# Ternary feed-forward stage: activations quantised in groups of two, two and four tiles in place of four and four

## The reference

```python
def act_quant(x):                      # per token
    scale = 128 / clip(max(abs(x), axis=-1), 1e-5)
    return clip(round(x * scale), -128, 127) / scale

def weight_quant(w):
    scale = 1 / clip(mean(abs(w)), 1e-5)
    return clip(round(w * scale), -1, 1) / scale

def bitlinear(x, w):   return act_quant(x) @ weight_quant(w).T
def h_bitlinear(x, w): return act_quant(fwht(x)) @ weight_quant(w).T   # fwht: Walsh-Hadamard transform

gate = bitlinear(x, w_gate)            # 1024 tokens, 256 -> 1024
up = bitlinear(x, w_up)
out = h_bitlinear(silu(gate) * up, w_down)
x = x + tanh(g_ffn[1]) * out           # here x on the right of bitlinear is the layernorm of x
```

## Time and profile before

| | us |
|---|---|
| median of 3 runs | 979.94 |
| lowest and highest of them | 978.31, 980.38 |
| the profiled execution | 978.6 |
| its span, first to last instruction | 976.9 |
| the ternary stage in it | 473.1 to 553.0 |

### The profile page before, as it was taken

How to read it: one execution, slowest core, us unless ns; L and a number is a source line. 1 busy time by engine, 2 the same in 40 slices (tenths; PEclk the granted TensorE clock), 3 DMA queues, 4 the chain that set the end, 5 groups by cost and what they waited for, 6 DMA issues and landing times. The chain is left out here.

```text
span 976.9 us, 17508 instructions
## 1 busy us (share of the span) xinstructions
PE 892.1 (91%) x5665; PEld 559.2 (57%) x5672; DVE 704.9 (72%) x1425; ACT 603.3 (62%) x1185; POOL 382.6 (39%) x325
## 2 busy tenths in 40 slices
PE   9799989898999999999499888999789999988868
PEld 4555646424777777776277663333455666666535
DVE  6999988889666676666778778997472334249777
ACT  5799945887777777777466376888414334213643
POOL 2899510586545555554133181000003776410010
PEclk9899999999999999999799999999899999999989
DMA  5333058000000000000000292000052332240001
GB/s 153 133 108 108 2 185 246 12 6 12 20 18 16 22 18 16 21 16 1 6 1 1 83 393 80 3 2 2 1 190 43 76 76 44 44 119 1 1 0 44
DMA packets 43975, 56.77 MB, mean 58 GB/s; under 512 B 5712, under 2 KB 34904, under 8 KB 43912
## 3 DMA queue, kind: packets, MB, share of 16 engines
q1 hardware_dynamic: 39880, 50.44, 15.7%
q0 software_dynamic: 4032, 5.51, 3.3%
HBM read 49.64 MB, written 6.23 MB: 57 GB/s over the span
## 5 line engine op out<-in xcount | busy, mean ns | idle before, releaser
L1511 POOL TENSOR_TENSOR a_scratch<-a_scratch,a_inverse 128x512 f32<-128x512 f32 x64 | 66.6, 1041 | 115.2 <-DVE a_inverse L1647 115.2
L2494 DVE TENSOR_REDUCE a_tops<-bank 128x4 f32<-128x1024 f32 x64 | 77.8, 1223 | 9.5 <-PE bank L2205 6.4
L2750 PE MATMUL bank<-wup,moe_xT 128*128 x184 | 83.0, 594 | 1.2 <-ACT moe_xT L2825 1.1
L2389 ACT ACTIVATE a_room<-bank,exp_scale 128x1024 f32<-128x1024 f32 x64 | 71.2, 1114 | 13.7 <-PE bank L2228 13.7
L587 POOL TENSOR_TENSOR ssm_drive<-ssm_du,ssm_b_row 128x1024 f32<-128x1024 f32 x32 | 74.5, 2355 | 3.4 <-DVE ssm_state L664 2.0
L1428 ACT ACTIVATE a_scratch<-bank,a_bias,a_q_factor 128x256 f32<-128x256 f32 x128 | 71.1, 560 | 7.1 <-DVE a_bias L1634 6.8
L664 DVE TENSOR_TENSOR_SCAN ssm_state<-bank,ssm_drive 128x512 f32<-128x512 f32 x64 | 74.6, 1207 | 0.8 <-POOL ssm_drive L587 0.5
L3018 DVE TENSOR_TENSOR moe_act_f<-bank,moe_silu 128x512 f32<-128x512 f32 x23 | 15.9, 691 | 76.7 <-ACT moe_silu L2832 65.0
L1240 PE MATMUL bank<-keys,a_scratch 128*128 (+1 forms) x256 | 69.1, 392 | 1.7 <-DVE xn L1574 0.7
L424 PE MATMUL bank<-ssm_seen,ident 128*128 128x512 f32 x124 | 63.7, 597 | 1.8 <-ACT ssm_seen L520 1.8
L2825 ACT COPY moe_xT<-bank 128x256 f32<-128x256 f32 x23 | 8.6, 373 | 91.9 <-PE bank L2738 74.5
(11 more groups left out here) (542 smaller groups left out, 2320.3 us busy)
## 6 DMA issues: line engine op xcount, KB each, us to landing
ssm_b_row<-ssm_b_spill SPq DMA_DIRECT2D x16, 512.0 KB, 3.7
wup<-in_l_up_dram SPq DMA_DIRECT2D x8, 1024.0 KB, 15.6
a_wq_in<-in_l1x_q_dram SPq DMA_DIRECT2D x32, 128.0 KB, 2.1
wdn<-in_l_down_dram SPq DMA_DIRECT2D x8, 512.0 KB, 8.1
keys<-in_l1x_o_dram SPq DMA_DIRECT2D x1, 2048.0 KB, 13.1
X<-in_x_dram SPq DMA_DIRECT2D x1, 1024.0 KB, 7.1
lora_raw<-in_l_gate_dram SPq DMA_DIRECT2D x1, 1024.0 KB, 4.8
lora_raw<-in_l_up_dram SPq DMA_DIRECT2D x1, 1024.0 KB, 6.9
```

The source lines that it names most:

```text
L1511: pool.tensor_tensor(prob[:, j, :, :], prob[:, j, :, :], inverse[:, j, :].unsqueeze(2).to_broadcast([P, 2, SEQ]), ALU.mult).then_inc(S["p_ ...
L2389: act.activation(prob[:, 2 * (f % 3) + p, :, :], bank[:, at:at + 2, :].rearrange("p j (t n) -> p (j t) n", t=2), ACT.Exp, scale=exp_scale[ ...
L2494: dve.tensor_reduce(tops[:, f // 2 % 3, :, first:first + 2].rearrange("p q h -> p h q"), bank[:, at:at + 2, :].rearrange("p h (q n) -> p h ...
L2750: last = pe.matmul(bank[:, 2 * (i % 2) + m, :], xT[:, i % 2, c, :], wup[:, bass.ds(e, 1), c * 2 * FF + m * FF:c * 2 * FF + (m + 1) * FF] . ...
```

## The change

`quantize` is called for three groups, tiles 0 and 1, tiles 2 and 3, and tiles 4 to 7, in place of two, tiles 0 to 3 and 4 to 7. `xq_scaled` therefore rises to 3, and the two waits for all groups, on ACT ahead of the loop and on DVE ahead of line 1999, ask for 3. ACT's wait for the first group, ahead of silu of unit 0, stays at 1; the factors of tiles 0 and 1 are what the first group makes.

```diff
                 silu_of(1)
-                act.wait_ge(xq_scaled, 2)
+                act.wait_ge(xq_scaled, 3)
                 for n in range(2 * NT):
...
-                quantize(0, halves[0])
-                quantize(1, halves[1])
-                dve.wait_ge(xq_scaled, 2)
+                for h, tiles in enumerate((range(0, 2), range(2, NT // 2), halves[1])):
+                    quantize(h, tiles)
+                dve.wait_ge(xq_scaled, 3)
                 chain(dve.tensor_scalar(out_scale[:, :], wback[:, 2:3], gate, 1.0 / 32, ALU.mult, ALU.mult))
```

## The result

The changed kernel takes 983.97 us at the median of 12 runs (982.65 to 985.92), against 979.99 for the kernel before in its 12 (978.31 to 982.52). The ratio is 1.0042, with a 95% interval of 1.0033 to 1.0052: **4.0 us slower**. The forecast was 981.2, with a range up to 983.2. It named the right wait and the right sign; the loss is three times as large as its 1.3.

The account below looks back on a forecast made before the run. The prediction took DVE's quantising to bound the ternary stage's head and PE its body. 0 from the head, +0.11 from the longer DVE queue and +1.2 for hold-ups gave +1.3 on 979.94: 981.2 us, range 979.0 to 983.2.

Parts of the forecast that it names:

- the right wait: ACT's wait for all groups' scale factors ahead of bring(0), claimed to delay transform(0) by 1.3 us.
- What bounds the head: Ternary stage's head: DVE's quantising is full; ACT's wait ahead of bring(0) costs nothing before, with 0.1 us to spare.
- First and second group: DVE's two groups of two tiles: 3.65 us each; the first xq starts 1.18 earlier.
- The 1.54: Start of DVE's third group, claimed to come 1.54 us later than the second group's start in the kernel before.
- Third group and the floor: Third signal at 485.33 without hold-up, so transform(0) starts at least 0.11 us later.
- The hold-up: POOL's products delaying DVE's third group: 0 to 2.2 us, taken as 1.2; hold-up case given chance 0.62.
- the first of the two worked orders: Third group on DVE: POOL holds an xn for 0.7 and line 1981 for 0.8, 1.5 us in all.
- the cheaper of the two orders: Third group on DVE: POOL's second product takes over at 484.30 and line 1990 loses 1.15 us.
- The clock: PE's granted clock around transform(0): up at about 484.6, before the standstill, with no cost in the sum.
- The case in which it costs something: Rival: PE's clock rises only behind 487.2, adding 1.6 to 3.2 us, 982.8 to 984.4; chance 0.12.
- No slack takes it back: After transform(0): PE runs without a gap of note, so the shift passes in full to the stage's end.
- The faster rival: Head's gain gets through bring(0) if the third signal comes before 484.3: down to -1.1 us, 978.8; chance 0.06.

Follow-up runs that it names:

- e4: Changed kernel with POOL's products of units 0 and 1 done on 8 of 512 columns, the rest zero-filled; median 978.75 us, ratio 1.0002, stage end 80.4.
- e3: Changed kernel with ten unread matmuls on PE between gate_and_up(2) and transform(0); median 980.06 us, ratio 1.0006, stage end 81.9.
- e5: Kernel before with the second group's maximum taken two times more; median 981.43 us, ratio 1.0018, stage end 83.5.
- e1: Changed kernel with ACT's wait for the third group's scale factors moved from ahead of bring(0) to n = 4; median 978.23 us, ratio 0.9991, stage end 79.6.
- e9: Repetition of e1 on another occasion; median 978.03 us, ratio 0.9992, stage end 79.5.
- e7: Changed kernel with the wait moved to n = 4 and eight unread matmuls on PE in the head; median 977.58 us, ratio 0.9991, stage end 78.0.

## Where the prediction held and where it failed

*What bounds the head.* Right. Moving the wait in the kernel before changed nothing, moving it in the changed kernel took the loss away.

*First and second group.* Right. Groups of two took 3.68 and 3.62 where 3.65 was worked out, the reduce 0.69. The price of a third group is seven instructions on DVE and not eight, as counted ahead of the result (x1432 against x1425 over the program): the factor takes three small ones. The 1.54 was read from whole groups, so that nothing hangs on the count. PE's first transposes came 3.22 behind the first xn in place of 4.37, 1.15 earlier, and gate_and_up(1) 7.48 in place of 8.63.

*Third group and the floor.* Right. It began 7.30 behind the first xn. With the 1.95 of hold-ups taken off, the signal stands at 12.22, the worked-out value; e4, which has all the waits and nearly none of the hold-ups, costs some 0.5.

*The hold-up.* The mechanism was right and the size was off: 1.2 taken, 1.95 measured (0.95 in the xn, 1.00 at line 1979). What came was the first of the two worked orders, priced at 1.5 there. POOL started its first product at 7.49, 0.19 behind the start of DVE's run of xn, and took 1.34, hardly longer than alone, while the run lost 0.95. I had left open whether POOL would wait out the run; it did not, and the second of the four xn waited for it. Then the second product met line 1979, 0.12 behind its own start, and that instruction lost a full 1.00. I took the value near the cheaper of the two orders, with no row that spoke for it; the row in the attention stage was of just this kind, an xn that lost 0.7 behind a POOL product, and 2.2 had been my upper end. "SBUF — State Buffer" of the Trainium skill, in its section "Who interferes with whom", has the winner keep the pair for its whole instruction: the trace agrees for one instruction (line 1979 ended at 486.12, POOL's product at 486.10), and shows beside it that a run of instructions on DVE did not keep POOL out.

*The clock.* **This is the step that failed.** The sum put PE's clock at nothing, and it measured 1.71. The case in which it costs something was there as a rival, with a chance of 0.12 and a price of 1.6 to 3.2, and the 982.8 to 984.4 that it gave take in the measured 983.97. That is luck in part, for its condition, a rise behind 487.2, did not come true. The reason I gave against it, that the clock is up before the standstill, was true (it was up at about 485.3) and was no reason: it fell again because of the standstill, as e3, e4 and e5 show. I had thought of a late rise alone. The trace of before held a row that shows the fall, between the two stages, where PE stands still for 7.74 us:

```profile
465.00:470.00 5.00, 2.49 (x18) 1.51 (x18) 3.91 (x14) 2.34 (x4) 0.00 (x0) 1.00 0.00 0
470.00:475.00 5.00, 0.00 (x0) 0.00 (x0) 4.33 (x17) 1.59 (x3) 0.00 (x0) 0.59 0.09 27
```

With 1.95 in place of 1.2 and 1.71 of clock in place of nothing, 0.11 + 1.95 + 1.71 = 3.77, which is what turn(1) and the barrier show (3.75 and 3.7).

*No slack takes it back.* Right: 3.75 at turn(1), 3.7 at the stage's end, with the body's units as long as before (turn(1) to turn(2) takes 3.16 and took 3.15). transform(0) came at 14.84, a little past the 13.0 to 14.6 that the forecast gave for it.

*The faster rival.* Its condition, a signal before 484.3 (11.2 behind the first xn), was put too late: to start at 10.55, as in e1, bring(0) would have needed it by then, and with no hold-up at all it stands at 12.22. Its price was wrong too. With the wait gone, 0.3 of the 1.15 came through, because gate_and_up(2) ran at half clock in e1 and in e9; in e7, with the clock up early, turn(1) came 1.87 earlier than in the kernel before.

## What to carry to other kernels

A change that brings the first piece of work forward by splitting a group makes the last piece later; look for the wait that asks for all pieces, and count how much it has to spare. If it has next to nothing, move it to its first user before splitting. When a forecast leaves TensorE idle between bursts, for 1.75 to 2.8 us in the cases here, give the next burst two prices, one at each clock, even where the clock has just come up; and when instructions of VectorE move in time, look anew at which of them now lie beside GpSimd's.

## What the runs showed of the hardware

A four-column tensor_scalar of DVE that starts beside a POOL product can last 1.17 us in place of 0.17, and a run of four xn 2.32 in place of 1.38, while POOL's product goes from 1.27 to 1.34. The granted clock fell to 0.50 for standstills of PE of 2.8, 2.3 and 1.75 us, 0 to 0.9 us after PE had gone on, and did not for one of 1.0. The rise moved against the program between two executions of the same kernel, from 11.5 to 12.7 in the kernel before and from 11.3 to 12.3 in the changed one.

The length of a standstill does not decide alone. Ahead of the attention stage PE stands for 3.27 us in the two profiles of the kernel before; behind that the clock from 177 to 179 us was 1.00 in the first and 0.50 in the second, and the same 16 matmuls took 1.69 us longer:

```profile
175.49 3.69 PE L1133 MATMUL bank<-keys 128*128 128x256 f32 x16 [3.27 <-PEq L787]
```
```profile
175.08 5.38 PE L1133 MATMUL bank<-keys 128*128 128x256 f32 x16 [3.27 <-PEq L787]
```

And the stages that nothing had touched differed from one execution to the next. The attention stage, ahead of the ternary one, took 297.5 to 297.6 in the five profiles in which the clock stayed up at that place, and 299.1 to 299.4 in the nine in which it fell. The stage behind the ternary one took 151.3 to 155.0. Differences of 1 to 2 us of this kernel are to be read in the stage and not in the median.
